# One burst of heads' outputs per group instead of two, in a causal attention and feed-forward layer on one core

## The reference, cut to what matters

```
q, k, v = x Wq + bq, x Wk + bk, x Wv + bv            (per head, 16 channels)
probs   = softmax(q k^T / 4 + causal mask)            (512 x 512 per head)
y       = probs v;  x1 = layernorm(x + y Wo + bo)
gate    = silu((x1 fp8(gate_w)) * gate_s);  up = (x1 fp8(up_w)) * up_s
out     = layernorm(x1 + ((gate * up) fp8(down_w)) * down_s)
```

## Time and profile before

| | us |
|---|---|
| Median of 3 runs (561.22 to 562.51) | 561.79 |
| The profiled execution's own time | 561.78 |
| Its span, first to last instruction | 560.0 |
| PE busy | 531.7 (95% of the span) |
| DVE busy | 458.7 (82%) |
| ACT busy | 315.2 (56%) |
| POOL busy | 226.5 (40%) |
| Chain that ended last, PE's share | 83% |
| Chain that ended last, DVE's share | 6% |

### The profile page before, as it was taken

The page is one execution under the profiler, slowest core; times in us unless marked ns, Lnnn a source line. Parts: engine busy times, 40 slices in busy tenths (PEclk is TensorE's granted clock), DMA queues, the critical chain, the costliest instruction groups (busy, mean ns, idle before and its releaser), DMA issues.

```text
span 560.0 us, 10677 instructions
## 1 busy us (share of the span) xinstructions
PE 531.7 (95%) x3921; PEld 356.8 (64%) x3921; DVE 458.7 (82%) x808; ACT 315.2 (56%) x579; POOL 226.5 (40%) x251
## 2 busy tenths in 40 slices
PE   8789899999999999999999999997899999999992
PEld 4345465665656656666666565563488888888892
DVE  7877588898988888889889898986748888888876
ACT  3046467666576675766766667664653554345530
POOL 5015233434443533434443453340425653455542
PEclk9888899999999999999999999997999999999997
DMA  5968665756554577556564664400000101110012
GB/s 181 262 165 271 162 181 156 179 187 172 175 172 128 183 198 199 164 135 187 157 173 153 139 200 152 123 4 2 1 0 1 39 1 39 39 38 27 12 39 75
DMA packets 61516, 68.19 MB, mean 122 GB/s; under 512 B 6296, under 2 KB 55832, under 8 KB 61464
## 3 DMA queue, kind: packets, MB, share of 16 engines
q1 hardware_dynamic: 60632, 66.59, 41.0%
q10 hardware_dynamic: 832, 0.92, 0.5%
HBM read 37.62 MB, written 29.61 MB: 120 GB/s over the span
## 4 chain that ended last, share of the span: by engine, by line
PE 83%; DVE 6%; issue 4%; DMA 3%; ACT 2%; POOL 1%; POOLq 0%; DVEq 0%; SPq 0%; ACTq 0%
PE ps L1110 16%; PE ps L964 11%; PE ps L972 10%; PE ps L859 10%; PE ps L1119 7%; PE ps L945 7%; PE ps L925 5%; PE ps L946 5%; PE ps L867 5%; PE ps L897 2%; DVE nmax L613 2%; PE ps L908 1%; PE ps L990 1%; DMA m_scratch<-mrow 1%; ACT probs L446 1%
## 5 line engine op out<-in xcount | busy, mean ns | idle before, releaser
L613 DVE TENSOR_REDUCE nmax<-ps 128x2 f32<-128x1024 f32 (+1 forms) x192 | 196.8, 1040 | 50.2 <-PE ps L946 49.7
L446 ACT ACTIVATE probs<-ps 128x512 f32<-128x512 f32 x320 | 183.9, 597 | 81.1 <-PE ps L964 79.8
L370 POOL TENSOR_SCALAR_AFFINE_SELECT probs<-probs 128x512 f32<-128x512 f32 x128 | 87.0, 693 | 213.1 <-ACT probs L446 213.1
L964 PE MATMUL ps<-q_st,k_st 98*128 98x384 bf16 (+3 forms) x512 | 123.6, 305 | 5.7 <-ACT probs L446 3.1
L397 POOL TENSOR_TENSOR f_l<-f_full,f_h 128x512 fp32r<-128x512 f32 x48 | 63.5, 1324 | 73.6 <-ACT f_h L529 73.6
L945 PE MATMUL ps<-k_st,q_st 98*128 98x256 bf16 (+2 forms) x384 | 83.0, 277 | 5.4 <-DMA k_st<-k_scratch 3.5
L946 PE MATMUL ps<-k_st,q_st 124*128 124x128 bf16 x512 | 84.7, 221 | 0.0
L972 PE MATMUL ps<-probs,v_st 128*32 128x512 f32 (+3 forms) x1024 | 83.9, 444 | 0.2
L964 PEld LDWEIGHTS ps<-q_st,k_st 98*128 98x128 bf16 x512 | 44.6, 99 | 51.1 <-issue 27.3
L524 ACT ACTIVATE sgate<-ps,s_gate 128x512 f32<-128x512 f32 x48 | 32.8, 685 | 60.0 <-PE ps L1110 60.0
L946 PEld LDWEIGHTS ps<-k_st,q_st 124*128 124x128 bf16 x512 | 46.2, 98 | 18.8 <-DVE nmax L613 13.7
(11 more groups left out here) (96 smaller groups left out, 832.9 us busy)
## 6 DMA issues: line engine op xcount, KB each, us to landing
q_st<-q_scratch SPq DMA_DIRECT2D x32, 384.0 KB
k_st<-k_scratch SPq DMA_DIRECT2D x32, 384.0 KB
q_scratch<-part SPq DMA_DIRECT2D x16, 384.0 KB, 3.7
k_scratch<-part SPq DMA_DIRECT2D x16, 384.0 KB, 2.6
xT<-in_attn_xT SPq DMA_DIRECT2D x8, 512.0 KB, 3.8
q_scratch<-part SPq DMA_DIRECT2D x16, 256.0 KB, 3.8
resid<-in_attn_x SPq DMA_DIRECT2D x8, 512.0 KB, 3.9
k_scratch<-part SPq DMA_DIRECT2D x15, 256.0 KB, 2.1
```

What stands on the lines that cost most here:

```text
L370: pool.affine_select(out=blocks, in_=blocks, compare_op=ALU.is_ge, fill=0.0, base=0, pattern=[*pattern, [1, P]], channel_multiplier=-1).th ...
L446: act.activation(probs[:, u, :], ps[:, u % 2, :], ACT.Exp, scale=SCALE).then_inc(exp_done, 1)
L613: dve.tensor_reduce(nmax[:, i, heads[0]:heads[-1] + 1], src, AX.X, ALU.max, negate=True).then_inc(max_taken, 1)
L964: m = pe.matmul(ps[:, u % 2, c0:c0 + T - P * j], k_st[0:RP, g, h, P * j:P * j + P], q_st[0:RP, g, h, P * j:T], start=True, stop=True)
```

## The change

The two bursts `attend_first` and `attend_rest` become one, `attend_all`, which stands where `attend_rest` stood: in the middle of the next group. Block 0's probabilities are therefore still needed while the next group's first four are written, so they get a tile with two halves (`probs_a`), and the other six units have a tile of their own (`probs_b`). The raw feed-forward weights use two tiles in place of three, and the third load, issued by SP, first waits until all 32 `quantize` steps of the first weight have run (of 96 in all).

```diff
-        w_raw = [sb(f"w_raw{m}", [P, KC * I]) for m in range(3)]
+        w_raw = [sb(f"w_raw{m}", [P, KC * I]) for m in range(2)]
...
-        probs = carve(NU * T).rearrange("p (u t) -> p u t", u=NU)
+        probs_a = carve(2 * HG * T).rearrange("p (z u t) -> p z u t", z=2, u=HG)
+        probs_b = carve((NU - HG) * T).rearrange("p (u t) -> p u t", u=NU - HG)
...
+        def prob_unit(w, u):
+            return probs_a[:, w % 2, u] if u < HG else probs_b[:, u - HG]
...
             def load_raw(m):
                 w, q = ((gate_w, KC), (up_w, KC), (down_w, IC))[m]
-                sp.dma_start(w_raw[m][:].rearrange("p (k n) -> p k n", k=q),
+                if m == 2:
+                    sp.wait_ge(quant, 8 * NQ // 3)
+                sp.dma_start(w_raw[m % 2][:].rearrange("p (k n) -> p k n", k=q),
...
             def exps(w, u):
                 if u == 0:
-                    wait(act, pv_done, 2 * (w - 1) + 1)
+                    wait(act, pv_done, w - 1)
                 if u == HG:
-                    wait(act, pv_done, 2 * (w - 1) + 2)
+                    wait(act, pv_done, w)
...
-            def attend_first(w):
-                pe.wait_ge(masked, 4 * w + 1)
+            def attend_all(w):
+                pe.wait_ge(masked, 4 * w + 4)
                 wait(pe, yn_ready, w)
                 pe.wait_ge(v_out, 2 * (w // G) + 2)
-                attend(w, 0).then_inc(pv_done, 1)
-
-            def attend_rest(w):
-                pe.wait_ge(masked, 4 * w + 4)
-                attend(w, 1)
-                attend(w, 2)
-                attend(w, 3).then_inc(pv_done, 1)
+                for j in range(TB - 1):
+                    attend(w, j)
+                attend(w, TB - 1).then_inc(pv_done, 1)
...
                     if w:
-                        attend_rest(w - 1)
+                        attend_all(w - 1)
...
                     scores(w, 9)
                     if more:
                         scores_max(w + 2, 4)
-                    attend_first(w)
                     if g == 0 and n:
                         transpose_yn(n - 1, 1, w)
                     if g == 3:
                         transpose_yn(n, 0, w if n + 1 < B else None)
                     if more:
                         scores_max(w + 2, 5)
-            attend_rest(W - 1)
+            attend_all(W - 1)
```

More of the change, by code:

```diff
@@ L82, in layer @@
         names = iter(("xT", "part", "rest", "q_st", "k_st", "v_st", "nmax", "mpart", "mrow",
-                      "probs", "yT", "rsum", "yn", "ynT",
+                      "probs_a", "probs_b", "yT", "rsum", "yn", "ynT",
                       "y_sum", "y_out", "hT_h", "hT_l", "sgate", "f_full", "f_h", "f_l"))
@@ L205, in attention_over @@
         def attention_over(eng):
-            for s, count in [(st_full, NU * W), (max_full, NM * W), (pv_done, 2 * W), (mT_full, W),
+            for s, count in [(st_full, NU * W), (max_full, NM * W), (pv_done, W), (mT_full, W),
                              (late_in, 16 * NLATE)]:
@@ L379, in _ @@
                     w, split = G * n + g, n + 1 < B and g in (0, 2)
-                    mask_units(w, 0, 3, probs[:, 0:HG, 0:P], [[0, HG]])
+                    mask_units(w, 0, 3, probs_a[:, w % 2, :, 0:P], [[0, HG]])
                     if split:
@@ L384, in _ @@
                         add_bias(n)
-                    mask_units(w, 4, 7, probs[:, HG:2 * HG, 0:P], [[0, HG]])
-                    mask_units(w, 4, 7, probs[:, HG:2 * HG, 3 * P:T], [[0, HG]])
-                    mask_units(w, 8, 9, probs[:, 2 * HG:NU, :].rearrange("p u (v t) -> p (u v) t", v=2)[:, :, 0:P], [[0, HG]])
+                    mask_units(w, 4, 7, probs_b[:, 0:HG, 0:P], [[0, HG]])
+                    mask_units(w, 4, 7, probs_b[:, 0:HG, 3 * P:T], [[0, HG]])
+                    mask_units(w, 8, 9, probs_b[:, HG:NU - HG, :].rearrange("p u (v t) -> p (u v) t", v=2)[:, :, 0:P], [[0, HG]])
                     if split:
@@ L442, in exps @@
                 if u == 0:
-                    wait(act, pv_done, 2 * (w - 1) + 1)
+                    wait(act, pv_done, w - 1)
                 if u == HG:
-                    wait(act, pv_done, 2 * (w - 1) + 2)
-                act.activation(probs[:, u, :], ps[:, u % 2, :], ACT.Exp, scale=SCALE).then_inc(exp_done, 1)
+                    wait(act, pv_done, w)
+                act.activation(prob_unit(w, u), ps[:, u % 2, :], ACT.Exp, scale=SCALE).then_inc(exp_done, 1)
             def empty_y(w):
-                act.wait_ge(pv_done, 2 * w + 2)
+                act.wait_ge(pv_done, w + 1)
                 wait(act, yt_full, w)
@@ L466, in _ @@
             for m in (0, 1):
-                mid_part(0, m, probs[:, m, :])
+                mid_part(0, m, probs_a[:, 0, m])
             dst = k_scratch[0:P]
@@ L553, in first_rest @@
                 dve.wait_ge(hi_ready, k + 1)
[L554 removed]
+                dve.scalar_tensor_tensor(probs_a[:, 0, k], ps[:, MX + k, :], (b_q, b_k)[k % 2][:, k // 2:k // 2 + 1],
                                          part[:, k, 0, :], ALU.add, ALU.subtract).then_inc(rest_ready, 1)
@@ L558, in first_lo @@
                 dve.wait_ge(mid_ready[k], 1)
-                dve.tensor_tensor(part[:, k, 2, :], probs[:, k, :], part[:, k, 1, :], ALU.subtract).then_inc(lo_ready[k], 1)
+                dve.tensor_tensor(part[:, k, 2, :], probs_a[:, 0, k], part[:, k, 1, :], ALU.subtract).then_inc(lo_ready[k], 1)
             def rest_part(n, k):
@@ L573, in quantize @@
                 c0, step = QC * (op // 8), op % 8
-                w = w_raw[m][:, c0:c0 + QC]
+                w = w_raw[m % 2][:, c0:c0 + QC]
                 to = (w_gate, w_up, w_down)[m][:, :, :].rearrange("p k n -> p (k n)")[:, c0:c0 + QC]
@@ L634, in empty_v @@
                 dve.wait_ge(v_full, n * 2 + v + 1)
-                wait(dve, pv_done, 2 * G * (n - 1))
+                wait(dve, pv_done, G * (n - 1))
                 dve.tensor_tensor(v_st[:, n % 2, 2 * v:2 * v + 2, :, 0:D],
@@ L972, in attend @@
                     m = pe.matmul(ps[HW * h:HW * h + HW, YB, P * j:T], v_st[:, (w // G) % 2, j, HG * g + h, :],
-                                  probs[:, u, c0:c0 + T - P * j], start=j == 0, stop=j == TB - 1)
+                                  prob_unit(w, u)[:, c0:c0 + T - P * j], start=j == 0, stop=j == TB - 1)
                 return m
-            def attend_first(w):
-                pe.wait_ge(masked, 4 * w + 1)
+            def attend_all(w):
+                pe.wait_ge(masked, 4 * w + 4)
                 wait(pe, yn_ready, w)
                 pe.wait_ge(v_out, 2 * (w // G) + 2)
-                attend(w, 0).then_inc(pv_done, 1)
-            def attend_rest(w):
-                pe.wait_ge(masked, 4 * w + 4)
-                attend(w, 1)
-                attend(w, 2)
-                attend(w, 3).then_inc(pv_done, 1)
+                for j in range(TB - 1):
+                    attend(w, j)
+                attend(w, TB - 1).then_inc(pv_done, 1)
             def transpose_h(n, c, bank):
```

## The result

The changed kernel took 579.33 us (median of 4 runs, 577.97 to 582.46), before 562.15 us (4 runs, 561.22 to 563.50). The ratio is 1.030, 95% interval 1.027 to 1.033: slower by 17.2 us. The forecast was 576.5, in the range of 567 to 582. The span of the profiled execution went from 560.0 to 578.1 us.

A forecast was written before the change was run, and what follows sets the result against it. PE was taken to pace the attention phase, with DVE close behind at 88%. Steady part +11.8 us plus the ends gave +15.1 on 561.78, that is 576.9, stated as 576.5 us; range 567 to 582.

The forecast's parts named there:

- The price of a burst: On PE, removing block 0 at the group's end frees 1.09 us; inside the middle burst it costs 0.88 us.
- DVE's times stay, counted from the middle burst: At the group's end DVE finishes no earlier, its times fixed behind the middle burst; PE's waits follow from them.
- The new starts on PE: Behind the removed burst, PE's next work starts only 0.25 to 0.42 us earlier per group; 0.5 us wait before unit 5 (g = 2).
- The sum per sequence: Four groups: 3.52 us paid, less 1.43 regained and 0.23 for one stall gone, net +1.86 us per sequence.
- The ends: Outside w = 2 to 28: +0.9 at the start, +1.8 at w = 28 and 29, +0.1 at w = 30, +0.5 last burst.
- From `take_max` 2 DVE runs without idle time: At the group's end DVE goes through take_max 2, normalize_y, quantize, take_max 3 and the MB read without pause.
- Only the first wait decides: Rival 1: at the group's end the second read of MB is ready when PE arrives; 572 us, chance 8%.
- The waits lower the clock: Rival 3: PE's idling of about 0.7 us per group makes the granted clock fall; 599 us, chance 4%.
- The saved drains come through: Rival 2: DVE is ready at unit 5, so 0.21 us per group is saved; 555.3 us, chance 10%.

The follow-up runs named there:

- two-filler kernel: Changed kernel plus two throwaway 512-column matmuls where block 0 had stood, between units 4 and 5 of the row maxima: 578.09 us, ratio 1.028.
- tiles-alone: Changed kernel with its new tiles and SP's wait, but the two bursts back in their old places on PE: 561.4 us, ratio 0.999.
- five fillers: Changed kernel plus five throwaway 512-column matmuls (about 1.08 us) where block 0 had stood: 586.97 us, ratio 1.044.
- the later rounding step: Changed kernel with DVE's rounding step between normalize_y and take_max 3 moved behind the second read of bank MB: 580.61 us, ratio 1.033.

## Why the prediction was right, step by step

- *The price of a burst.* Forecast: 0.88 us for block 0 inside a burst; measured 160.64 - 159.75 = 0.89.
- *DVE's times stay, counted from the middle burst.* Shown by the rows after for g = 2, to 0.01 us. In g = 0 `take_max` 3 came a little earlier, 4.87 us behind the burst for 4.96 before (184.72 - 179.76), and that group lost less than forecast (0.35 or 0.46 us for 0.47).
- *The new starts on PE.* Work at 6.38 forecast and 6.37 measured for g = 2. The two-filler kernel shows the wait ahead of unit 5 by experiment and not only by its bracket.
- *The sum per sequence.* +1.86 forecast, 47.80 - 45.85 = +1.95 measured. From w = 2 to w = 28 the forecast was 11.8 and the measurement 13.66 - 0.84 = 12.8, 1 us more. By kind of group, over these 26 steps: 0.5 too little was forecast for g = 2, 0.2 for g = 1 and 0.7 for g = 3, and 0.4 too much for g = 0. Of the 0.7, 0.4 fell on the last step, ahead of w = 28, where PE waited for the DMA. After two other g = 3 groups PE waited for DVE's read of the value projection (0.36 us at 133.01 and 0.47 us at 324.23 by their brackets).
- *The ends.* This is the mis-sized term: +3.3 forecast, 18.1 - 12.8 = +5.3 in the profiled execution. Three parts make the 2.0. At the start 0.84 came that was put at nothing, with PE at the lower clock behind its wait for the DMA. At w = 28 the burst cost 1.7 more at the lower clock, which the prediction allowed for only at the second burst behind it, and only in its upper bound. From w = 29 on, 0.5 less was lost than forecast (1.9 for 2.4). Why the clock fell at w = 28 is open, as said above. So part of this miss belongs to the one profiled execution.
- *From `take_max` 2 DVE runs without idle time.* As a statement on the rows of g = 2 right, as a cause wrong there. Moving a step out of that stretch or cutting all steps to a quarter left `take_max` 3 at 4.70 us behind the burst: its start is set by PE's delivery of unit 3. Only in g = 0 did DVE's own chain set it, by 0.17 us. The forecast did not depend on which of the two it is, since PE's delivery too lies at a fixed distance behind the middle burst. That was luck.
- *The rivals.* "Only the first wait decides" is out: the second wait (0.2 us) is in the rows. "The waits lower the clock" is out in the steady part (1.00), and the lower clock came only at the ends. "The saved drains come through" is out here. The two prices of block 0 that it rests on, 1.09 us apart and 0.89 inside a burst, are in the rows; that a kernel gets the difference back is not shown.

So the cause is this. The block 0 burst lay in a gap of PE that the round trip unit 3, `take_max` 3, unit 5 leaves in each group. Taken out, it freed 1.09 us, of which PE could use 0.26 to 0.50 (a group's growth taken from the 0.85 us by which its burst, 1.46 us before and 2.31 after, is longer); put into the middle, it cost its full 0.88. That the gap is real, and that the place of block 0 alone matters, is shown by the tiles-alone and the two-filler kernels. What stays open: the last 0.1 us per sequence that five fillers cost less than expected, whether the longer waits for `split_max` are all that the later rounding step added, and why the clock fell at w = 28 in one profile.

## What to carry to other kernels

Work between two units of a double-buffered ring may be the only thing that hides the other engine's turn. Before moving it, measure how late that engine would be without it: end of its instruction, counted from an event that does not move, against the time at which the waiting engine would now arrive. Then price the new place separately. Here a longer burst also left the consumer without data for longer: DVE's idle time ahead of `take_max` 2 went from 0.46 to 0.84 us. If fillers no longer than the wait cost nothing, the wait is real.

## What was not expected of the hardware

Two kernels that differ by two filler matmuls per group ran the same group (w = 28) at a mean granted clock of 0.86 in one profile and 1.00 in the other, and at the lower level the burst cost 1.7 us more. Two other kernels had waits as long or longer just ahead of the same burst (0.52 and 0.90 us, 0.52 and 1.22 us) and kept 1.00. Otherwise the float32 bursts behaved as their rows before had said: 0.89 us for 512 columns in four column strips of the array.
